# Normalising the finished rows while the last expert still runs, in a decoder layer with mixture of experts

## The chip, the cores and the metric
The kernel runs on one core of a Trainium2 chip. The time is device microseconds (us) of one execution. TensorE (PE) multiplies matrices, with the weight loads listed apart (PEld); VectorE (DVE), ScalarE (ACT) and GpSimd (POOL) do element work; SyncE (SP) issues transfers. POOL also issues the indirect transfers (gather and scatter by a list of row numbers). Engines wait on each other by semaphores only.

## The reference, cut to what matters
64 sequences of 128 tokens, width 256, so 8192 rows. Self attention, residual and layer norm; cross attention, residual and layer norm; then a mixture of experts:

```
probs = softmax(x @ Wr + br); gates, ids = top_k(probs, 2)      # 8 experts, 2 for each token
cap = ceil(1.2 * 8192 / 8) = 1229                                # rows of one expert, by gate, best first
xg = x[disp_tok].reshape(8, cap, 256)
h = silu(xg @ W1 + b1); out = h @ W2 + b2                        # 256 -> 1024 -> 256
y = zeros.at[disp_tok].add(out * gate)
x = layernorm(x + y)                                             # eps 1e-5, no scale or shift
```

A row can be added to by two experts, and by none when both are full. The final norm of a row needs the sum of all its experts.

## The kernel before, in words
The kernel is a row of blocks, and every block ends with all engines meeting. The attention block writes its rows twice to memory: into `rows` (to gather from) and into `total` (to add to). `logits_block` makes the router's logits. `route_block` finds each expert's 1229 rows: a softmax and the two best, a search in 15 steps for each expert's threshold gate (DVE, ACT and PE in turn), running counts, and then in 8 batches one-hot matrices `hit_row` and `hit_lane` whose products give the list `ids`. At its end POOL gathers the first 10 tiles of 128 rows (expert 0, its three chunks) into `xg` (L1292).

`experts_block` takes 8 experts with 3 chunks each (3, 3 and 4 tiles of 128 rows; 384, 384 and 462 rows), 24 chunks in all. Numbers in 32 bits are split into a rounded part and a rest, so each product is three matmuls. TensorE's order for each chunk (L1465 and after) is: transposes of the next chunk (L1448), `up` of this one (48 matmuls), `down` of the chunk before (24 matmuls for each tile of 128 rows). Its last piece is `down` of chunk 23. ACT rounds the transposed rows (L1502), makes silu twice for each of 8 slices (L1531, L1532), and rounds the next expert's weights (L1510). DVE makes the rests (L1559 for rows, L1565 for weights, L1572 for the hidden layer), adds the bias to the result (`take_o`, L1582) and multiplies by the gate (L1587). Two PSUM buffers hold results of `down`, so TensorE's third tile waits until DVE has taken the first. POOL gathers the chunk three ahead (L1623) and adds the finished chunk into `total` by an indirect transfer with addition (`scatter`, L1639). Experts' scatters stay in order, since two may add to the same row.

`norm_block` starts when every scatter has landed. SP loads `total` in 16 groups of 512 rows (L1677), DVE makes the statistics (L1709, L1704), POOL in four small instructions the factor and the shift (L1692 to L1697), ACT normalises 64 tiles (L1718), SP stores 16 groups (L1681).

Of the kernel before, what the change touches and what calls it, by code (L numbers as in the profile page):

```python
# [4 lines left out]
FP32 = mybir.dt.float32  # L5
# [7 lines left out]
P = 128  # L13
# [948 lines left out]
def route_block(nc, tiles, cap, logits, rows_dram, ids, first_weights, first_rows, consts):  # L962
# [7 lines left out]
    PARTS = tiles // BATCH  # L970
    DVE_TAGS = 4
    Q = 2 * tiles
# [3 lines left out]
    with ExitStack() as c:  # L976
# [16 lines left out]
        ident = sb("ident", [P, P])  # L993
# [41 lines left out]
        hit_lane = sb("hit_lane", [P, Q, P], FP16)  # L1035
        hit_row = sb("hit_row", [P, Q, ROWS], FP16)
        tagged = sb("tagged", [P, Q, ROWS], FP16)
# [6 lines left out]
        w1_in, w2_in, w_in = first_weights  # L1044
        xg, x_loaded = first_rows
# [12 lines left out]
        dve_tags = sem("dve_tags")  # L1058
        routed = sem("routed")
# [3 lines left out]
        def _(sp):  # L1063
# [3 lines left out]
            sp.dma_start(w1_in[:], consts["w1"][0:1].rearrange("a (t p) n -> p (a t) n", p=P)).then_inc(w_in, 16)  # L1067
            sp.dma_start(w2_in[:], consts["w2"][0:1].rearrange("a (t p) n -> p (a t) n", p=P)).then_inc(w_in, 16)
# [6 lines left out]
        def _(act):  # L1075
# [3 lines left out]
            nc.scalar.activation(warm[:], dummy[:], ACT.Sign)  # L1079
            act.wait_ge(split, 1)  # L1080
# [7 lines left out]
            for b in range(Q // BATCH):  # L1088
                part, kth = divmod(b, 2)
                if b % DVE_TAGS == DVE_TAGS - 1:  # L1090
                    continue
                act.wait_ge(rows_hit, b + 1)
                for t in range(part * BATCH, (part + 1) * BATCH):
                    q = kth * tiles + t
                    ins = nc.scalar.activation(tagged[:, q, :], hit_row[:, q, :], ACT.Copy, scale=tag[:, t:t + 1])
                ins.then_inc(tags_made, 1)

        @block.tensor
        def _(pe):
# [5 lines left out]
            last.then_inc(pe_done, 1)  # L1105
            for i in range(STEPS):
# [13 lines left out]
            for b in range(Q // BATCH):  # L1120
# [5 lines left out]
                for t in range(part * BATCH, (part + 1) * BATCH):  # L1126
                    q = kth * tiles + t
                    last = nc.tensor.matmul(bi[:, part, :], hit_lane[:, q, :], tagged[:, q, :],
                                            start=(b % 2 == 0 and t == part * BATCH),
                                            stop=(b % 2 == 1 and t == (part + 1) * BATCH - 1))  # L1130
            last.then_inc(pe_done, 1)

        @block.vector
        def _(dve):
# [11 lines left out]
            _, parts, _, _, _ = chunks_of(cap)  # L1146
            v.memset(xg[:, :, parts[-1] - 1, :], 0.0).then_inc(cleared, 1)
            v.memset(ones[:], 1.0)
            v.memset(base[:], 0.0)
            v.memset(ones_h[:], 1.0)  # L1150
            for i in range(STEPS):
                for j in range(3):
                    ins = v.memset(third[:, i, j:j + 1], (j + 1) * step_of(i) - half_unit(i))
            link(ins)
            v.tensor_copy(tries[:], third[:, 0, :])
            link(v.tensor_copy(ahead[:], third[:, 1, :]))

# [30 lines left out]
            dve.wait_ge(pe_done, 1)  # L1188
            v.tensor_copy(gt[:], bt[:]).then_inc(split, 1)
# [69 lines left out]
            for b in range(Q // BATCH):  # L1259
                part, kth = divmod(b, 2)  # L1260
                qs = slice(kth * tiles + part * BATCH, kth * tiles + (part + 1) * BATCH)
                v.tensor_tensor(hit_row[:, qs, :], row_h[:, qs].unsqueeze(2).to_broadcast([P, BATCH, ROWS]),
                                iota_h[:, 0:ROWS].unsqueeze(1).to_broadcast([P, BATCH, ROWS]), ALU.is_equal).then_inc(rows_hit, 1)
                v.tensor_tensor(hit_lane[:, qs, :], lane_h[:, qs].unsqueeze(2).to_broadcast([P, BATCH, P]),
                                iota_h[:].unsqueeze(1).to_broadcast([P, BATCH, P]), ALU.is_equal).then_inc(lanes_hit, 1)
                if b % DVE_TAGS == DVE_TAGS - 1:
                    dve.wait_ge(rows_hit, b + 1)
                    v.tensor_tensor(tagged[:, qs, :], hit_row[:, qs, :],
                                    tag[:, part * BATCH:(part + 1) * BATCH].unsqueeze(2).to_broadcast([P, BATCH, ROWS]),
                                    ALU.mult).then_inc(dve_tags, 1)  # L1270
            dve.wait_ge(pe_done, 4)
# [23 lines left out]


XG = 4
AHEAD = XG - 1


def chunks_of(cap):
# [545 lines left out]
```

## Time and profile before

| | us |
|---|---|
| three runs | 1637.54, 1636.06, 1637.61 (median 1637.54) |
| the profiled execution, its own time | 1637.37 |
| its span, first to last instruction | 1635.6 |
| start of the block of the experts | 1097.6 |
| start of the block of the norm | 1586.4 |

The profile counts its times from the start of the span. An engine's line in a timeline gives the start, the busy time, the engine, the line of the kernel, the operation with what it writes and reads, and how many of them are merged; brackets tell how long the engine had been idle and what ended that. "issue" is a wait for nothing that the profile shows. A line of SPq is a transfer being issued, not its landing.

### The profile page before, as it was taken

Reading aid. Unit: us, or ns where it says so; the run is one execution under the profiler, and the core shown is the slowest. Engines: PE = TensorE matmul, PEld = TensorE weight load, DVE = VectorE, ACT = ScalarE, POOL = GpSimd, SP = SyncE. Lnnn points to the kernel's source line nnn. Section 1 sums busy time; section 2 is a strip of 40 time slices with the busy share of each in tenths; the row PEclk is TensorE's granted clock in tenths of the full one; section 3 lists DMA queues with packets and bytes.
Section 4 is the critical chain, followed back from the end, with each engine's and each line's share of the span. In section 5 each row is a group of like instructions: output and inputs, shape, how many; then the busy total and the mean of one; then the engine's idle time right before and its main releaser. Section 6 shows DMA issues by size and latency. Waiting matters only on the chain. (4 is left out here: it accounts for less than half of the span.)

```text
span 1635.6 us, 43777 instructions
## 1 busy us (share of the span) xinstructions
PE 1412.0 (86%) x17886; PEld 1188.3 (73%) x17886; DVE 1021.5 (62%) x2276; ACT 1015.4 (62%) x1555; POOL 598.8 (37%) x607
## 2 busy tenths in 40 slices
PE   7999999999999999999998560119999999999940
PEld 5777777777777777777776340119999999999940
DVE  5666666666777777777777368955455445445425
ACT  4677777777777777777766352337555456556407
POOL 2645454544433232323230000032455445545236
PEclk9999999999999999999999885559999999999975
DMA  6112122221212222222221451013443444343139
GB/s 189 33 49 62 58 61 60 60 60 60 61 60 73 79 80 78 80 67 82 70 69 45 139 165 15 1 44 82 95 104 47 97 94 95 53 99 48 22 78 355
DMA packets 128006, 129.53 MB, mean 79 GB/s; under 512 B 26496, under 2 KB 114672, under 8 KB 127808
## 3 DMA queue, kind: packets, MB, share of 16 engines
q1 hardware_dynamic: 112704, 106.24, 21.3%
q0 software_dynamic: 15104, 20.48, 7.7%
q8 instruction: 144, 2.36, 0.6%
q14 instruction: 54, 0.44, 0.1%
HBM read 82.53 MB, written 44.16 MB: 77 GB/s over the span
## 5 line engine op out<-in xcount | busy, mean ns | idle before, releaser
L515 ACT ACTIVATE at_pr<-at_A 128x2048 f32<-128x2048 f32 x128 | 240.7, 1880 | 147.2 <-PE at_A L335 147.2
L610 DVE TENSOR_REDUCE at_mx<-at_A 128x12 f32<-128x1536 f32 x128 | 224.6, 1754 | 56.3 <-PE at_A L300 52.7
L35 PE MATMUL ex_D<-ex_w,ex_hT 128*128 128x256 f32 (+1 forms) x1920 | 234.2, 282 | 0.3
L35 PEld LDWEIGHTS ex_D<-ex_w,ex_hT 128*128 128x128 f32 (+1 forms) x1920 | 231.0, 184 | 2.9 <-DVE ex_raw L1582 1.8
L35 PE MATMUL ex_U<-ex_xT,ex_w 128*128 128x384 f32 (+1 forms) x1152 | 224.6, 354 | 3.4 <-DVE ex_xT L1559 3.4
L1639 POOL DMA_INDIRECT total<-ex_o,ids x80 | 131.4, 1642 | 237.1 <-DVE ex_o L1587 220.1
L35 PEld LDWEIGHTS ex_U<-ex_xT,ex_w 128*128 128x128 f32 x1152 | 208.4, 190 | 12.1 <-issue 3.8
L755 POOL TENSOR_SCALAR_AFFINE_SELECT at_pr<-at_pr 128x2048 f32<-128x2048 f32 x64 | 128.5, 2007 | 205.2 <-ACT at_pr L515 205.1
L1572 DVE TENSOR_TENSOR ex_hT<-ex_h,ex_hT 128x384 fp32r<-128x384 f32 (+1 forms) x192 | 112.6, 587 | 100.2 <-ACT ex_hT L1532 90.8
L646 DVE TENSOR_TENSOR at_oT<-at_C,at_oT 128x512 fp32r<-128x512 f32 x64 | 44.2, 691 | 165.3 <-ACT at_oT L528 165.3
L335 PE MATMUL at_A<-at_qp,at_kt 32*128 32x256 f32 x2048 | 139.8, 388 | 0.0
L350 PE MATMUL at_C<-at_pr,at_v 128*32 128x128 f32 x4096 | 138.4, 276 | 1.0 <-ACT at_oq L522 1.0
L350 PEld LDWEIGHTS at_C<-at_pr,at_v 128*32 128x32 f32 x4096 | 104.0, 110 | 43.3 <-issue 42.1
L1531 ACT ACTIVATE ex_h<-ex_U,ex_b 128x384 f32<-128x384 f32 (+1 forms) x192 | 115.9, 604 | 26.7 <-PE ex_U L35 21.4
L1502 ACT CAST ex_xT<-ex_T 128x384 fp32r<-128x384 f32 (+1 forms) x48 | 21.8, 506 | 161.8 <-PE ex_T L1448 161.7
L1532 ACT ACTIVATE ex_hT<-ex_U,ex_b 128x384 fp32r<-128x384 f32 (+1 forms) x192 | 114.3, 595 | 0.0
L762 POOL TENSOR_SCALAR at_shift<-at_mv 128x2 f32<-128x2 f32 x64 | 14.8, 231 | 265.2 <-DVE at_mv L674 262.7
L35 PE MATMUL at_B<-at_wo,at_oT 128*128 128x256 f32 x768 | 108.1, 290 | 1.4 <-DVE at_oT L646 1.4
L1582 DVE TENSOR_TENSOR ex_raw<-ex_D,ex_b 128x256 f32<-128x256 f32 x80 | 33.8, 423 | 118.6 <-PE ex_D L35 118.2
L35 PE MATMUL at_B<-at_wv,at_sT 128*128 128x256 f32 x768 | 106.7, 288 | 0.0
L35 PE MATMUL at_B<-at_sT,at_wk 128*128 128x512 f32 x384 | 105.0, 409 | 0.6 <-ACT at_qp L484 0.6
L1623 POOL DMA_INDIRECT xg<-rows,ids x70 | 92.2, 1318 | 24.1 <-issue 20.1
(219 smaller groups left out, 2690.1 us busy)
## 6 DMA issues: line engine op xcount, KB each, us to landing
w_in<-in_w SPq DMA_DIRECT2D x16, 1024.0 KB
at_turned<-in_x_turned SPq DMA_DIRECT2D x16, 512.0 KB, 4.6
at_x<-in_x SPq DMA_DIRECT2D x16, 512.0 KB, 4.1
x<-at_y SPq DMA_DIRECT2D x32, 256.0 KB, 2.4
at_x<-x SPq DMA_DIRECT2D x16, 512.0 KB, 3.8
at_turned<-in_ctx_turned SPq DMA_DIRECT2D x16, 512.0 KB, 4.8
rows<-at_y SPq DMA_DIRECT2D x32, 256.0 KB, 2.2
total<-at_y SPq DMA_DIRECT2D x32, 256.0 KB, 3.0
```

What stands on the lines that cost most here:

```text
L35: last = nc.tensor.matmul(out, pick_l(left, a), pick_r(right, b), start=(start and n == 0), stop=(stop and n == 2))
L335: last = nc.tensor.matmul(A[:, i, n, :, :], kt[rows, g % 2, half, tok], qp[rows, g % 2, half, :, tok], start=False, stop=(n == 1), skip_gr ...
L350: last = nc.tensor.matmul(b[32 * j:32 * j + VW, (2 * n + quad) * P:(2 * n + quad + 1) * P], v[:, g % 2, 2 * np_ + n, half * HEADS_HALF + 4 ...
L515: nc.scalar.activation(pr[:, k % 2].rearrange("p i n a q -> p (i n a q)"), A[:].rearrange("p i n a q -> p (i n a q)"), ACT.Exp).then_inc(e ...
L610: nc.vector.tensor_reduce(mx[:, k % 2, 0:12], A[:, 0:3].rearrange("p i n a k -> p (i n a) k"), AX, ALU.max).then_inc(max_done, 1)
L646: nc.vector.tensor_tensor(oT[:, u % 2, 1].rearrange("p t n -> p (t n)"), C[1][:, :], oT[:, u % 2, 0].rearrange("p t n -> p (t n)").bitcast ...
L755: nc.gpsimd.affine_select(out=t, in_=t, compare_op=ALU.is_ge, fill=0.0, base=0, pattern=[[0, 16], [1, P]], channel_multiplier=-1).then_inc ...
L1531: nc.scalar.activation(h[:, m % HR, 0:n], U[m % UP][:, 0:n], ACT.Silu, bias=b1[:, j, m:m + 1])
L1532: nc.scalar.activation(hT[:, par(j, ch), 0, m, 0:n], U[m % UP][:, 0:n], ACT.Silu, bias=b1[:, j, m:m + 1]).then_inc(u_done, 1)
L1572: nc.vector.tensor_tensor(hT[:, par(j, ch), 1, m, 0:n], h[:, m % HR, 0:n], hT[:, par(j, ch), 0, m, 0:n].bitcast(FP32), ALU.subtract).then_ ...
L1623: nc.gpsimd.indirect_dma_start(xg[0:n, xg_of(s), b, :], None, rows_dram, bass.IndirectOffsetOnAxis(ap=ids[0:n, e, at:at + 1], axis=0), bou ...
L1639: nc.gpsimd.indirect_dma_start(sum_dram, bass.IndirectOffsetOnAxis(ap=ids[0:n, e, at:at + 1], axis=0), o[0:n, pr, b, :], None, bounds_chec ...
```

## The change
1. The norm's block is gone. Its work stands in the block of the experts. As soon as the scatters of expert 6 have landed (`sum_complete`), SP loads groups 0 to 7 of `total` into eight places (four in the weights' input buffers, two in `o`, two new) and POOL gathers the last expert's own 10 tiles of rows from `total`. The other eight groups are loaded one by one into places whose store has landed. Groups are laid out with four rows side by side in a partition. The groups hold the last expert's rows too, at values that are not final; they are stored and overwritten later.
2. The last expert's results are not scattered into `total`: DVE adds bias, multiplies by the gate and adds to the gathered row (`take_own`), takes statistics of these rows apart, and mixes the statistics of the groups between its pieces.
3. POOL makes the factors, and itself normalises groups 0 to 3; ACT groups 4 to 15 and the own rows. When all 16 stores have landed, POOL scatters the 10 own tiles into `out` (now with 128 spare rows).
4. Expert 0's start stands in `route_block`: weights, biases and the mask are loaded, rounded and split there, and the first chunk is gathered, transposed, rounded and given its gates there. Only two chunks (6 tiles) are gathered in that block; the third follows in the next. Constants are set by POOL and not by DVE at the block's start. The one-hot matrices lie in a ring of 4 batches and no longer all at once; DVE waits before it writes a batch for the products of the batch four before.
5. Weights and the shared buffers are allocated for both blocks. TensorE's `up` and `down` keep their order; the transposes of chunk 0 are what is moved.

```
+            act.wait_ge(sh["w_in"], 32)
+            for src, dst, _ in weights:
+                nc.scalar.copy(dst[:, 0], src[:]).then_inc(sh["w_hi"], 1)
...
+            for k, (src, dst, _) in enumerate(weights):
+                dve.wait_ge(sh["w_hi"], k + 1)
+                v.tensor_tensor(dst[:, 1], src[:], dst[:, 0].bitcast(FP32), ALU.subtract).then_inc(sh["w_lo"], 1)
+            dve.wait_ge(sh["small_in"], 48)
+            dve.wait_ge(x_loaded[0], 16 * parts[0])
...
-            for s in range(AHEAD):
+            for s in range(ROUTED):
...
+            def load_bulk(g):
+                sp.dma_start(space(g), sum_dram[g * G:(g + 1) * G, :].rearrange("(p b) n -> p b n", p=P)).then_inc(bulk_in[g % len(spaces)], 16)
+
+            sum_complete(sp)
+            for g in range(len(spaces)):
+                load_bulk(g)
+            for g in range(groups):
+                if g < POOL_GROUPS:
+                    sp.wait_ge(bulk_made_pool, g + 1)
+                else:
+                    sp.wait_ge(bulk_made_act, g - POOL_GROUPS + 1)
+                sp.dma_start(out_dram[g * G:(g + 1) * G, :].rearrange("(p b) n -> p b n", p=P), space(g)).then_inc(early_stored[g] if g < again else late_stored, 16)
+                if g > 0 and g - 1 < again:
+                    sp.wait_ge(early_stored[g - 1], 16)
+                    load_bulk(g - 1 + len(spaces))
...
+            def take_own(ch, bulk):
+                e, j = E - 1, (E - 1) % 2
+                dve.wait_ge(own_in[ch], 16 * parts[ch])
+                dve.wait_ge(gate_ready, e * NC + ch + 1)
+                for b, (_, n) in enumerate(tiles_of[ch]):
+                    at = tiles_before(e, ch) + b
+                    dve.wait_ge(d_full, at + 1)
+                    if b == 0:
+                        wait(dve, own_sum, starts[ch])
+                    nc.vector.tensor_tensor(raw[0:n, b, :], Dn[(starts[ch] + b) % 2][0:n, :], b2[0:n, j, :], ALU.add).then_inc(d_done, 1)
+                    dve.wait_ge(d_done, at + 1)
+                    nc.vector.scalar_tensor_tensor(total_rows(ch, b, n), raw[0:n, b, :], gate[0:n, ch, b:b + 1], total_rows(ch, b, n),
+                                                   ALU.mult, ALU.add).then_inc(own_sum, 1)
+                    bulk_statistics(*bulk[b])
...
+                    elif ch == 1:
+                        rest_h(e, j, ch)
+                        take_own(0, ((0, 4), (4, 8), (8, 12)))
+                        own_statistics(0)
+                    else:
+                        for m in range(HT):
+                            rest_h(e, j, ch, m, m + 1)
+                            bulk_statistics(12 + m, 13 + m)
+                        take_own(1, ((20, 24), (24, 28), (28, 32)))
+                        own_statistics(1)
+                        take_own(2, ((32, 36), (36, 40), (40, 44), (44, tiles)))
+                        own_statistics(2)
...
+            sum_complete(pool)
+            for ch in range(NC):
+                free = (E - 1) * NC + ch
+                pool.wait_ge(t_full, free * 2)
+                pool.wait_ge(gate_ready, free)
+                for b, (_, n) in enumerate(tiles_of[ch]):
+                    at = starts[ch] + b
+                    nc.gpsimd.indirect_dma_start(total_rows(ch, b, n), None, sum_dram,
...
             for g in range(groups):
...
+                pool.wait_ge(bulk_stats, g + 1)
+                rates(g * NB, NB, bulk_rates)
+                if g < POOL_GROUPS:
+                    pool.wait_ge(bulk_rates, g + 1)
+                    for b in range(NB):
+                        t = g * NB + b
+                        ins = nc.gpsimd.tensor_scalar(space(g)[:, b, :], space(g)[:, b, :], rstd[:, t:t + 1], shift[:, t:t + 1],
+                                                      ALU.mult, ALU.add)
+                    ins.then_inc(bulk_made_pool, 1)
+                for ch in range(NC - 1):
+                    if g == OWN_AFTER[ch]:
+                        own_rows(ch)
+            own_rows(NC - 1)
+            for g in range(again):
+                pool.wait_ge(early_stored[g], 16)
+            pool.wait_ge(late_stored, 16 * (groups - again))
+            for ch in range(NC):
+                pool.wait_ge(own_made, ch + 1)
...
+                    nc.gpsimd.indirect_dma_start(out_dram, bass.IndirectOffsetOnAxis(ap=ids[0:n, E - 1, at:at + 1], axis=0),
+                                                 total_rows(ch, b, n), None, bounds_check=out_dram.shape[0] - 1).then_inc(own_stored, 16)
+            pool.wait_ge(own_stored, 16 * LT)
```

Here POOL_GROUPS is 4, OWN_AFTER is (4, 7), ROUTED is 2, `again` is 8 (16 groups, 8 places).

## Rows read from the trace of the kernel before

**Rows 1.** Busy time by stage: start:end, length, busy of each engine, granted clock, DMA share, GB/s

```profile
1105.40:1571.60 466.20, 465.85 (x3226) 454.64 (x3226) 227.09 (x453) 256.87 (x445) 211.32 (x143) 0.99 0.37 74
1571.60:1586.40 14.80, 0.00 (x0) 0.00 (x0) 1.47 (x5) 0.00 (x0) 6.16 (x4) 0.59 0.28 33
1586.40:1635.60 49.20, 0.00 (x0) 0.00 (x0) 26.81 (x128) 32.10 (x64) 27.22 (x65) 0.50 1.02 342
```

**Rows 2.** Timeline at the start of the routing block

```profile
976.34 0.63 ACT L1078 ACTIVATE rt_probs<-rt_probs 128x512 f32<-128x512 f32 x1 [7.08 <-DMA rt_limits<-in_limits]
992.28 0.63 ACT L1081 ACTIVATE rt_low<-rt_gt 128x512 f32<-128x512 uint16 x1 [15.22 <-DVE rt_gt L1189]
```

**Rows 3.** Timeline from the end of routing to the first product of expert 0

```profile
1080.81 0.24 DVE L1280 TENSOR_TENSOR ids<-rt_id_sum,rt_empty 128x80 int32<-128x80 f32 x1
1082.09 1.32 POOL L1292 DMA_INDIRECT xg<-rows,ids  x1 [162.52 <-SPq L976]
1094.26 1.03 POOL L1292 DMA_INDIRECT xg<-rows,ids  x1 [0.30 <-issue]
1097.63 3.70 ACT L1510 CAST ex_w<-w_in 128x2048 fp32r<-128x2048 f32 x2 [23.85 <-PEq L976]
1099.56 4.49 DVE L1565 TENSOR_TENSOR ex_w<-w_in,ex_w 128x2048 fp32r<-128x2048 f32 x2 [18.50 <-ACT ex_w L1510]
1099.70 3.04 POOL L1623 DMA_INDIRECT xg<-rows,ids  x1 [0.30 <-issue]
1100.50 1.54 PE L1448 MATMUL ex_T<-ex_ident,xg 128*128 128x128 f32 x6 [23.15 <-DMA ex_ident<-in_ident]
1103.04 1.90 POOL L1623 DMA_INDIRECT xg<-rows,ids  x1 [0.30 <-issue]
1104.28 1.01 DVE L1559 TENSOR_TENSOR ex_xT<-ex_T,ex_xT 128x384 fp32r<-128x384 f32 x2
1105.43 6.56 PE L35 MATMUL ex_U<-ex_xT,ex_w 128*128 128x384 f32 x24 [3.39 <-DVE ex_xT L1559]
```

**Rows 4.** Timeline of the last expert: scatters and one instruction of each kind

```profile
1531.18 1.73 POOL L1639 DMA_INDIRECT total<-ex_o,ids  x1 [0.30 <-issue]
1532.87 8.69 PE L35 MATMUL ex_D<-ex_w,ex_hT 128*128 128x256 f32 x72
1552.94 0.64 DVE L1572 TENSOR_TENSOR ex_hT<-ex_h,ex_hT 128x462 fp32r<-128x462 f32 x1 [0.62 <-ACT ex_hT L1532]
1568.81 0.42 DVE L1582 TENSOR_TENSOR ex_raw<-ex_D,ex_b 128x256 f32<-128x256 f32 x1 [2.42 <-PE ex_D L35]
1573.08 1.56 POOL L1639 DMA_INDIRECT total<-ex_o,ids  x1 [6.08 <-DVE ex_o L1587]
1578.67 1.48 POOL L1639 DMA_INDIRECT total<-ex_o,ids  x1 [0.31 <-issue]
1586.46 19.35 SPq L1677 DMA_DIRECT2D nm_x<-total  x16
```

**Rows 5.** Timeline of the norm: one group on DVE, POOL and ACT, and the stores

```profile
1592.17 1.37 DVE L1709 BATCH_NORM_STATS2 nm_stats<-nm_x 128x6 f32<-128x256 f32 x4
1592.44 0.24 POOL L1692 TENSOR_SCALAR nm_shift<-nm_mv 128x4 f32<-128x4 f32 x1 [5.86 <-DVE nm_mv L1704]
1593.58 0.38 DVE L1704 BATCH_NORM_AGGREGATE nm_mv<-nm_stats 128x2 f32<-128x6 f32 x4
1594.42 32.10 ACT L1718 ACTIVATE nm_x<-nm_x,nm_shift,nm_rstd 128x256 f32<-128x256 f32 x64 [41.51 <-POOL nm_shift L1697]
1594.47 0.24 POOL L1692 TENSOR_SCALAR nm_shift<-nm_mv 128x4 f32<-128x4 f32 x1
```

**Rows 6.** POOL's costliest groups in the span: count, then busy us and mean ns

```profile
L755 POOL TENSOR_SCALAR_AFFINE_SELECT at_pr<-at_pr 128x2048 f32<-128x2048 f32 x64 | 128.5, 2007 | 205.2 <-ACT at_pr L515 205.1
L746 POOL TENSOR_TENSOR at_sT<-at_turned,at_sT 128x1024 fp32r<-128x1024 f32 x32 | 76.4, 2387 | 53.3 <-DVE at_m L620 35.4 <-ACT at_sT L471 17.9
```

**Rows 7.** Chain that ended last: start, length, what

```profile
1586.46 3.95 DMA nm_x<-total
```

More of the change, by code:

```diff
@@ L959, in _, with route_block @@
             take(groups - 1)
-def route_block(nc, tiles, cap, logits, rows_dram, ids, first_weights, first_rows, consts):
+def route_block(nc, tiles, cap, logits, rows_dram, ids, sh, consts):
     LT = -(-cap // P)
@@ L970, in route_block @@
     PARTS = tiles // BATCH
+    _, parts, starts, widths, tiles_of = chunks_of(cap)
     DVE_TAGS = 4
+    RING = 4
     Q = 2 * tiles
@@ L1092, in _ @@
                 act.wait_ge(rows_hit, b + 1)
-                for t in range(part * BATCH, (part + 1) * BATCH):
-                    q = kth * tiles + t
-                    ins = nc.scalar.activation(tagged[:, q, :], hit_row[:, q, :], ACT.Copy, scale=tag[:, t:t + 1])
+                for k in range(BATCH):
+                    t = part * BATCH + k
+                    ins = nc.scalar.activation(tagged[:, b % RING, k, :], hit_row[:, b % RING, k, :], ACT.Copy, scale=tag[:, t:t + 1])
                 ins.then_inc(tags_made, 1)
+            for half in range(HALVES):
+                act.wait_ge(sh["t_full"], half + 1)
+                nc.scalar.copy(xT[:, 0, 0, half, :widths[0]], T[half][:, 0:widths[0]]).then_inc(sh["x_hi"], 1)
         @block.tensor
@@ L1125, in _ @@
                     pe.wait_ge(dve_tags, (b + 1) // DVE_TAGS)
[L1126 to L1131, printed above, removed]
+                for k in range(BATCH):
+                    last = nc.tensor.matmul(bi[:, part, :], hit_lane[:, b % RING, k, :], tagged[:, b % RING, k, :],
+                                            start=(b % 2 == 0 and k == 0), stop=(b % 2 == 1 and k == BATCH - 1))
+                last.then_inc(batch_done, 1)
+            pe.wait_ge(x_loaded[0], 16 * parts[0])
+            for half in range(HALVES):
+                for k, (off, n) in enumerate(tiles_of[0]):
+                    last = nc.tensor.matmul(T[half][:, off:off + n], xg[0:n, 0, k, half * P:(half + 1) * P], ident[0:n, 0:n],
+                                            start=True, stop=True, is_transpose=True)
+                last.then_inc(sh["t_full"], 1)
         @block.vector
@@ L1145, in _ @@
             v = nc.vector
[L1146 to L1156, printed above, removed]
             link(v.tensor_reduce(col[:], logits[:], AX, ALU.max))
@@ L1297 @@
 XG = 4
+NC_CHUNKS = 3
 AHEAD = XG - 1
+ROUTED = 2
+POOL_GROUPS = 4
+OWN_AFTER = (4, 7)
+SPARE = 2
 def chunks_of(cap):
     LT = -(-cap // P)
-    NC = 3
+    NC = NC_CHUNKS
     used = cap + cap % 2
@@ L1341, in experts_block @@
-        gate = sb("gate", [P, NC, NB])
         raw = sb("raw", [P, NB, D])
         o = sb("o", [P, 2, NB, D])
-        ident = sb("ident", [P, P])
-        T = [c.enter_context(nc.psum_tensor(f"ex_T{i}", [P, G], FP32)) for i in range(2)]
+        groups = tiles // NB
+        stats = sb("stats", [P, tiles + LT, 6])
+        mv = sb("mv", [P, tiles + LT, 2])
+        rstd = sb("rstd", [P, tiles + LT])
+        shift = sb("shift", [P, tiles + LT])
+        minus_half = sb("minus_half", [P, NB])
@@ L1394, in landed, with space, total_rows, own_at @@
             return 16 * sum(parts[t % NC] for t in range(s % 2, s + 1, 2))
+        def space(g):
+            return spaces[g % len(spaces)]
+        def total_rows(ch, b, n):
+            return xg[0:n, xg_of((E - 1) * NC + ch - 1), b, 0:D]
+        def own_at(ch):
+            return tiles + starts[ch]
+        def sum_complete(eng):
+            last = (E - 1) * NC - 1
+            for s in (last - 1, last):
+                eng.wait_ge(added[s % 2], landed(s))
         def gathered(s):
@@ L1641, in scatter @@
                                                  compute_op=ALU.add).then_inc(added[pr], 16)
-            for s in range(E * NC):
+            for s in range(ROUTED, AHEAD):
+                gather(s)
+            nc.gpsimd.memset(minus_half[:], -0.5).then_inc(half_made, 1)
+            for s in range((E - 1) * NC + 1):
                 if s + AHEAD < E * NC:
```

281 lines of the change are left out of this document (159 added, 122 removed).

## The prediction

> **What bounds the kernel now.** I read the busy time by stage first. From 1105.4 to 1571.6 us PE is busy 465.85 of 466.20 us; nothing in the experts can be gained except work of PE itself, and the change removes none. Behind it come two stages without PE: 14.8 us to the norm (only 6.16 us of POOL in them) and 49.2 us of norm with the DMA engines full (share 1.02, 342 GB/s) [rows 1]. That is 64.0 us after PE's end, for 16.8 MB of loads and stores and one scatter. In the experts' stage the DMA share is 0.37, DVE is busy 49%, ACT 55% and POOL 45%: there is room for the norm beside PE, if the sums are complete early enough. The timeline before the experts comes next: `ids` are done at 1081.05, PE's first product starts at 1105.43, 24.4 us later. In them POOL issues ten gathers, all engines meet, and ACT, DVE and PE prepare expert 0 in turn [rows 3].
>
> **Part A, the start of expert 0.** At the front of routing nothing is gained: ACT's exponential waits for the tenth constant's landing at 976.34, whatever DVE clears before [rows 2]. POOL's constants stand beside that. The two rounding copies (3.70 us [rows 3]) move to ACT between 976.97 and 992.28, when it was idle for 15.2 us [rows 2]; if the weights came over 11 us late there, the search would start late. The ring's wait costs nothing as long as PE stays less than three batches behind DVE, which the busy PE of those products cannot miss: I count 0, bounds 0 and +1.
> After `ids`: before, ten gathers from 1082.09 to 1095.29, then the meeting, 2.34 us until ACT starts at 1097.63 [rows 3]. After the change six gathers. The steps of their pitch are (1094.26 - 1082.09)/9 = 1.35 us, but DVE now splits the weights (4.49 us) at 1081.1 to 1085.6, and beside just this work two gathers took 3.04 and 1.90 us and not 1.0 [rows 3]. So: two gathers until about 1086.6, four more to 1092.0. The third ends at 1088, its rows are there some 2 us later, six transposes (1.54), the last rounding (0.5) and the rests (1.01) [rows 3] end at 1092.8. The meeting, 2.3 us: PE's first product at 1095.1 instead of 1105.4. I take **-10.5 us** (1094.9). Bounds: gathers not held by DVE and the meeting at 1090.3 give -12.3; all six held for 0.3 us more each, -8.5. The four gathers of the third chunk now stand at the front of the next block, to 1100.3. PE has the first chunk's 48 products before it asks for them (24 of them took 6.56 us [rows 3]), so they are in time by some microseconds. The second expert's weights wait for them too, with most of an expert's length in hand.
> The Trainium skill, SBUF — State Buffer, section Who interferes with whom, says that a VectorE instruction with two SBUF inputs holds off a GpSimd instruction that reads SBUF until it ends. The 3.04 us agree with it. By it POOL's four normalised groups and DVE's rests (both inputs in SBUF) would hold each other off too, by at most 8 x 0.6 = 5 us in the stage below; the sum goes without.
>
> **Part B, the tail.** Times here are those of the profile before; part A shifts them all.
> 1. The sums are complete when expert 6's last scatter has landed. Its issue ends at 1531.18 + 1.73 = 1532.9. The last scatter of all ended at 1580.15 and the next block began at 1586.46 [rows 4]; less the 2.3 us of a meeting [rows 3] it landed 4.0 us after. So 1536.9.
> 2. POOL gathers ten own tiles: 10 x 1.35 + 0.8 for waits = 14.3 us, to 1551.2. The first three land at about 1544.2 (issue 4.3, landing 3, an estimate between the 2 us above and the 4.0).
> 3. PE stalls. DVE takes `down` of chunk 21 only with the own rows there; PE's 72 products start at 1532.87, at 2.9 us for a tile [rows 4], and the third tile waits from 1538.6 to 1544.6. That is 6 us, and the granted clock was down to 0.59 on average in the stage after PE's end [rows 1], so some 2 us more after it. It is later held by DVE again and ends near 1579.7, 8 us late. It does not set the end, by the next steps.
> 4. DVE from 1544.2: 26.8 us for 16 groups of statistics [rows 1], own statistics 10 x 0.44 = 4.4 [rows 5], bias and multiply-add 10 x 0.84 = 8.4 and eight rests 8 x 0.64 = 5.1 [rows 4]: 44.7 us, to 1589 without gaps, 1591.7 with those where a tile of PE is late. Group 15 is done before its own last four tiles, at 1589.8.
> 5. POOL from 1551.2, once group 0's statistics are there at 1546.7. One set of four small instructions has a pitch of 1594.47 - 1592.44 = 2.03 us [rows 5]; 19 sets are 38.4. Normalising on POOL is not in the trace. Bounds: 0.25 us a tile (2007 ns / 8) and 0.60 (2387 / 4) [rows 6], I take 0.35, nearer the first, which also has one tile as input: 16 x 0.35 + 0.3 = 5.9. POOL ends its last set at 1595.4, two us behind group 15's at 1593.4.
> 6. ACT: a tile is 32.10 / 64 = 0.50 us [rows 5]; group 15 at 1595.4, its store issued and landed 4.4 us later (3.95 for the first load [rows 7]): 1599.8. The own last tiles are ready at 1597.4. The loads of groups 8 to 15 hang on stores 0 to 7; they are issued by 1586 and do not bind. The 16.8 MB need 49 us at 342 GB/s [rows 1] and have 63.
> 7. POOL's ten scatters wait for all stores. With addition the pitch is (1578.67 - 1573.08)/3 = 1.86 us [rows 4]; the gather without it has 1.35. A plain scatter is in no row: bounds 1.31 and 1.86, I take 1.40, as only the addition divides them: 14.0, to 1613.8. Landing 3.9 as in step 1: **1617.7**.
> So the tail ends 1635.6 - 1617.7 = 17.9 us earlier. Both parts: 1635.6 - 17.9 - 10.5 = 1607.2 of span; the profiled execution is 1.8 us over its span, **1609.0 us**. It stands 0.2 us under the median of the three runs, so that is a gain of 28.5 us on the median, 1.7%.
>
> **Rivals.**
> (a) The own rows come late. The gathers share the DMA engines with eight loads of 512 KB, which fill them for 12 us at 342 GB/s. If they land behind these (own rows at 1553, not 1544), DVE becomes the bound: its 44.7 us from there give 1598 for group 15, 5.3 + 4.4 us on to the stores, scatters from 1607.7: **1617**. Half way, 1614. For it: the gathers of 3.04 us [rows 3] show that POOL's transfers can be held. Against: the stores of the same queue come only later. The Trainium skill, DMA: Bandwidth & Descriptors, section Queues, rings and completion order, says that an engine serves its queues in turn, by packets; that speaks for the shorter landing, and no row here shows the two side by side.
> (b) The plain scatter costs as much as the adding one: + 10 x 0.46 = 4.6 us, **1613.6**. With POOL's tiles at 0.60 another 4, 1617.6.
> (c) The changed start gives nothing, as the meeting waits for something else (the third gather's rows, or code): **1619.5**.
> (d) Slower: POOL is the serial engine of the new tail, and all 16 tiles that it normalises stand before every other step of it. Each us more for a tile costs 16 us at the end. At 2.2 us a tile (a small instruction, POOL held off by DVE) the sum is 1609 + 16 x 1.85 = **1638.6**; it decides from 2.15. Against: 2048 elements took 2.0 us while DVE ran beside [rows 6], and this is 256.
> (e) That the change does not do what it says: TensorE's order is said to be changed, and in the code it stays. Nothing is priced for it; it is no case of its own.
>
> **How the numbers follow.** The forecast 55%, (a) 18%, (b) 15%, (c) 6%, (d) 3%, 3% for something faster: POOL's tiles at 0.25, gathers not held, a landing of 2 us give 1609 - 1.6 - 1.8 - 1.9 = 1603.7. The bounds of the unknown costs together reach from there to 1609 + 4 + 4.6 + 5 + 2 = 1624.6. The range is 1602 to 1624. About 0.2%, 3.3 us, is what a measurement of this kernel can tell from no change: faster 0.95, the same 0.01, slower 0.04.
>
> **What would show it.** In the profile after: PE's first product 10 us earlier, with six gathers before it, the first two long; a hole in PE of some 6 us in the last expert, with a lower granted clock behind it, and PE's end 8 us later in its stage; POOL busy without a gap from there to its last set, then a wait for the stores of 4 to 5 us, then ten scatters at 1.3 to 1.9 us, which end the chain. Step 4 is wrong if the chain runs through DVE's statistics, step 6 if through ACT or the stores' loads. The whole is wrong if POOL's tiles take over 1 us.

## The result, and the profile after

| | before | after |
|---|---|---|
| median | 1636.8 us (4 runs, 1636.03 to 1637.61) | 1614.8 us (4 runs, 1612.23 to 1615.79) |
| ratio | | 0.9863, 95% interval 0.9846 to 0.988 |
| the profiled execution, its own time | 1637.37 | 1615.76 |
| its span | 1635.6 | 1614.0 |

The gain is 22.0 us (28.5 were forecast); the forecast was 1609.0 us with a range of 1602 to 1624. A repeat in a later measurement gave 1614.03 us beside 1637.91.

The attention stage takes a few us more or less from one execution to the next: the first load of the routing block starts at 970.27 us in the profile before, at 972.33 in the one after and at 968.42 in the repeat. So times of different executions are compared from that load and written with a plus: +123.8 is 123.8 us after it. By this clock before ends at +665.3, after and its repeat at +641.7 both.

The busy time by stage of the kernel after, columns as in [rows 1]: the experts to PE's end, then to the first scatter into `out`, then to the end.

```profile
1096.10:1571.70 475.60, 466.97 (x3226) 454.99 (x3226) 250.34 (x553) 264.28 (x462) 246.54 (x210) 0.99 0.41 96
1571.70:1594.80 23.10, 0.00 (x0) 0.00 (x0) 11.39 (x54) 20.92 (x42) 16.38 (x38) 0.56 0.85 313
1594.80:1614.00 19.20, 0.00 (x0) 0.00 (x0) 0.00 (x0) 0.00 (x0) 9.92 (x10) 0.50 0.19 66
```

PE has the same work (466.97 us against 465.85) and 8.6 us of holes. Behind its end stand 42.3 us and not 64.0 [rows 1]; in the first 23.1 of them ACT is the busy engine (20.92 us), in the last 19.2 only POOL issues.

The timeline of the kernel after from `ids` to the first product of expert 0 answers to [rows 3].

```profile
1082.79 0.24 DVE L1289 TENSOR_TENSOR ids<-rt_id_sum,rt_empty 128x80 int32<-128x80 f32 x1
1082.94 4.49 DVE L1292 TENSOR_TENSOR ex_w_even<-ex_w_in,ex_w_even 128x2048 fp32r<-128x2048 f32 x2
1084.06 2.35 POOL L1321 DMA_INDIRECT ex_xg<-rows,ids  x1 [108.56 <-issue]
1086.71 1.62 POOL L1321 DMA_INDIRECT ex_xg<-rows,ids  x1 [0.30 <-issue]
1088.63 1.01 POOL L1321 DMA_INDIRECT ex_xg<-rows,ids  x1 [0.30 <-issue]
...
1091.44 1.54 PE L1146 MATMUL ex_T<-ex_ident,ex_xg 128*128 128x128 f32 x6 [12.13 <-DMA ex_xg<-rows,ids]
1092.57 1.01 POOL L1321 DMA_INDIRECT ex_xg<-rows,ids  x1 [0.30 <-issue]
1092.89 1.20 DVE L1301 TENSOR_TENSOR ex_xT<-ex_T,ex_xT 128x384 fp32r<-128x384 f32 x2 [1.00 <-ACT ex_xT L1108]
1096.11 1.30 PE L35 MATMUL ex_U<-ex_xT,ex_w_even 128*128 128x384 f32 x3 [3.13 <-PEq L978]
```

`ids` to PE's first product: 13.1 us, before 24.4. Two gathers run beside DVE's split of the weights and take 2.35 and 1.62 us, the others 1.01; the sixth ends at 1093.58, and the meeting is over 2.5 us later. The transposes and rests lie beside the last gathers.

The tail of the kernel after, from its timelines, in order of start; this answers to [rows 4, 5].

```profile
1522.99 1.73 POOL L1803 DMA_INDIRECT total<-ex_o,ids  x1 [0.30 <-issue]
1526.76 1.75 SPq L1523 DMA_DIRECT2D ex_w_in<-total  x4
1527.56 1.12 POOL L1822 DMA_INDIRECT ex_xg<-total,ids  x1 [2.85 <-issue]
1530.33 1.01 POOL L1822 DMA_INDIRECT ex_xg<-total,ids  x1 [0.30 <-issue]
1536.68 0.42 DVE L1718 TENSOR_TENSOR ex_raw<-ex_D,ex_b 128x256 f32<-128x256 f32 x1 [10.16 <-DMA ex_xg<-total,ids]
1537.16 4.54 PE L35 MATMUL ex_D<-ex_w_odd,ex_hT 128*128 128x256 f32 x24 [6.62 <-issue]
1539.54 1.02 POOL L1822 DMA_INDIRECT ex_xg<-total,ids  x1 [0.30 <-DVE ex_mv L1697]
1542.97 2.18 POOL L1849 TENSOR_SCALAR ex_w_in<-ex_w_in,ex_rstd,ex_shift 128x256 f32<-128x256 f32 x4
1547.52 3.26 POOL L1849 TENSOR_SCALAR ex_w_in<-ex_w_in,ex_rstd,ex_shift 128x256 f32<-128x256 f32 x4
1551.68 20.00 PE L35 MATMUL ex_D<-ex_w_odd,ex_hT 128*128 128x256 f32 x168
1562.53 2.08 ACT L1642 ACTIVATE ex_o<-ex_o,ex_shift,ex_rstd 128x256 f32<-128x256 f32 x4 [9.48 <-POOL ex_shift L1836]
1584.33 1.41 DVE L1692 BATCH_NORM_STATS2 ex_stats<-ex_spare 128x6 f32<-128x256 f32 x4 [2.25 <-DMA ex_spare<-total]
1590.97 2.07 ACT L1634 ACTIVATE ex_xg<-ex_xg,ex_shift,ex_rstd 128x256 f32<-128x256 f32 x4
1594.81 1.15 POOL L1863 DMA_INDIRECT out<-ex_xg,ids  x1 [3.87 <-issue]
1606.50 0.97 POOL L1863 DMA_INDIRECT out<-ex_xg,ids  x1 [0.30 <-issue]
```

To be seen: the last scatter of expert 6 ends at 1524.72, and SP is released at 1526.76. The third own gather ends at 1531.34, its rows are there at 1536.66. PE stands for 6.62 us, and the 24 matmuls behind the hole take 4.54 us where 2.9 is usual [rows 4]. ACT gets its first group at 1562.53. The first scatter stands at 1594.81, ten take 12.66 us, and the span ends 6.5 us behind the last one.

What PE does in and behind that hole, from the busy time by stretch (start:end, length, PE busy, granted clock, DMA share, GB/s):

```profile
1530.54:1537.16 6.62, 0.00 (x0) 0.73 1.02 394
1537.16:1541.54 4.38, 4.38 (x24) 0.63 1.02 399
```

The granted clock was 1.00 in the stretch before the hole, 0.63 on average in the 4.38 us behind it, and 1.00 again from 1541.54 on. So the slow 24 matmuls go with a lower clock, as forecast.

The end of the chain of waits of the kernel after (start, us, what):

```profile
1574.71 0.21 POOL ex_shift L1836
1574.92 0.03 issue
1574.94 8.09 ACT ex_w_in L1642 x16
1583.03 4.01 ACT ex_o L1642 x8
1587.04 4.01 ACT ex_spare L1642 x8
1591.05 0.02 issue
1591.07 2.67 DMA out<-ex_spare
```

Up to 1574.9 the chain runs through POOL, from there through ACT without a gap. The prediction had named this, the chain through ACT, as the sign that its step 6 is wrong. POOL's groups in the span of the kernel after (busy us, mean ns, idle before) answer to the bounds of [rows 6]:

```profile
L1849 POOL TENSOR_SCALAR ex_w_in<-ex_w_in,ex_rstd,ex_shift 128x256 f32<-128x256 f32 x16 | 10.4, 660 | 0.4
L1822 POOL DMA_INDIRECT ex_xg<-total,ids x10 | 10.3, 1025 | 5.6 <-issue 5.3 <-DVE ex_mv L1697 0.3
L1863 POOL DMA_INDIRECT out<-ex_xg,ids x10 | 9.9, 992 | 6.6 <-issue 6.6
```

### The profile page after: what moved, and what is told of

Same layout as the page of the kernel before. It is cut to its first block and busy times, and to the rows that moved or that the text cites. A ratio compares the mean times of both kernels' runs of the same rounds, so it can differ in the third digit from the quotient of the medians.

```text
span 1614.0 us, 43834 instructions
## 1 busy us (share of the span) xinstructions
PE 1415.6 (88%) x17886; PEld 1190.3 (74%) x17886; DVE 1026.1 (64%) x2246; ACT 1011.6 (63%) x1549; POOL 621.5 (39%) x696
## 5 line engine op out<-in xcount | busy, mean ns | idle before, releaser
L755 POOL TENSOR_SCALAR_AFFINE_SELECT at_pr<-at_pr 128x2048 f32<-128x2048 f32 x64 | 128.4, 2007 | 205.2 <-ACT at_pr L515 205.2
L1803 POOL DMA_INDIRECT total<-ex_o,ids x70 | 115.8, 1655 | 197.3 <-DVE ex_o L1736 182.4
L35 PE MATMUL ex_D<-ex_w_odd,ex_hT 128*128 128x256 f32 (+1 forms) x960 | 118.3, 284 | 6.9 <-issue 6.6
L35 PEld LDWEIGHTS ex_D<-ex_w_odd,ex_hT 128*128 128x128 f32 (+1 forms) x960 | 116.6, 186 | 8.2 <-issue 6.8
L35 PE MATMUL ex_D<-ex_w_even,ex_hT 128*128 128x256 f32 (+1 forms) x960 | 117.2, 281 | 1.0 <-DVE ex_raw L1731 0.9
L35 PEld LDWEIGHTS ex_D<-ex_w_even,ex_hT 128*128 128x128 f32 (+1 forms) x960 | 115.2, 184 | 2.7 <-DVE ex_raw L1731 2.2
L35 PE MATMUL ex_U<-ex_xT,ex_w_even 128*128 128x384 f32 (+1 forms) x576 | 113.5, 356 | 3.8 <-PEq L978 3.1
L35 PEld LDWEIGHTS ex_U<-ex_xT,ex_w_even 128*128 128x128 f32 x576 | 104.9, 191 | 8.6 <-issue 3.5
L35 PE MATMUL ex_U<-ex_xT,ex_w_odd 128*128 128x384 f32 (+1 forms) x576 | 111.0, 351 | 0.0
```

The source lines that it names most:

```text
L35: last = nc.tensor.matmul(out, pick_l(left, a), pick_r(right, b), start=(start and n == 0), stop=(stop and n == 2))
L755: nc.gpsimd.affine_select(out=t, in_=t, compare_op=ALU.is_ge, fill=0.0, base=0, pattern=[[0, 16], [1, P]], channel_multiplier=-1).then_inc ...
L1803: nc.gpsimd.indirect_dma_start(sum_dram, bass.IndirectOffsetOnAxis(ap=ids[0:n, e, at:at + 1], axis=0), o[0:n, pr, b, :], None, bounds_chec ...
```

## The experiments

Three measurements of four kernels each, every one with runs of the kernel before beside them, to which the ratios refer; the kernel after stood at 0.9863 and in the first of these measurements at 0.9856 (0.9841 to 0.9871; called the repeat below). Experiments 1 to 3 were measured beside the repeat, 4 to 7 and 8 to 11 later; their medians are set against its 1614.03 us too, and the kernel before had 1637.91, 1637.13 and 1636.35 us in the three.

The traces have a width of their own. In kernels that are the same up to there, the issue of expert 6's last scatter ends at +552.2 to +552.5 in four traces (after, repeat, experiments 8 and 9) and at +553.5 to +553.7 in five (2, 3, 4, 5 and 7). Of a later end in these five, about 1.2 us stood there before the tail began.

**1. The start alone.** Part A as in the change, with the norm's block and the last expert's end as before.

```
-            sum_complete(sp)
-            for g in range(len(spaces)):
-                load_bulk(g)
...
-            sum_complete(pool)
...
+            scatter(E * NC - 1)
...
+    norm_block(nc, tiles, total, out)
```

> Only the changed start of expert 0 (point 4 of the change); the norm is its own block again after the last scatter, as in the kernel before. Theory: the start is worth 11.4 us from the routing block's first instruction to the first product of expert 0 (123.8 us in the profile after, 135.2 before), of which 1.1 are lost again in the first expert, so 1636.8 - 10.3 = 1626.5 us, and the distance from the last product to the end is 64 us as before. Rival (c), the start gives nothing: 1637. A third reading, that the start is worth less and the tail more than the forecast said: between, 1630.

Measured: 1628.19 us, ratio 0.9944 (0.9929 to 0.9959). Part A is worth 9.7 us (10.5 forecast), and the tail 14.2 more (to the repeat's 1614.03), where 17.9 were forecast. The expectation of 1626.5 was 1.7 us too low. In the traces the way from the routing block's first load to the first product is 123.7 us here, 123.8 in the change and 135.2 before: 11.4 us. Some of it is lost again in the first expert, where PE waits for ACT's `ex_hT` and DVE's `ex_raw`: PE has holes of 1.20, 0.52 and 0.90 us here, 0.63 and 0.89 in the profile after, 0.60 in the repeat, none before.

**2. Twice as many groups on POOL.**

```
-POOL_GROUPS = 4
-OWN_AFTER = (4, 7)
+POOL_GROUPS = 8
+OWN_AFTER = (8, 10)
```

> POOL normalises 8 groups instead of 4 (and ACT 8 instead of 12); own rows' factors come after groups 8 and 10. Theory that POOL's serial chain sets the tail: 16 more tiles of 0.55 to 0.8 us, so the end comes 9 to 13 us later, about 1625 us. Rival, DVE's statistics and the loads they wait for set the tail: those have 3 us in hand, so up to 1618. Rival, ACT sets it: ACT has 16 tiles less, so the same or 2 us faster, 1613.

Measured: 1623.77 us, 0.9914 (0.9899 to 0.9929): 9.7 us dearer than the repeat of the change for 16 tiles more, 0.61 us a tile. Two lines of its timeline, POOL's last tiles and ACT's first:

```profile
1575.32 2.16 POOL L1849 TENSOR_SCALAR ex_spare<-ex_spare,ex_rstd,ex_shift 128x256 f32<-128x256 f32 x4
1579.52 2.07 ACT L1642 ACTIVATE ex_w_in<-ex_w_in,ex_shift,ex_rstd 128x256 f32<-128x256 f32 x4 [26.60 <-POOL ex_shift L1836]
```

ACT, which needs 0.50 us a tile and has time, waits 26.6 us for the factors that stand behind POOL's tiles. In these 16 tiles more, what POOL normalises stays on the path with its full price.

**3. The last wait on SP.** SP and not POOL waits for the ten scatters into `out`.

```
-            pool.wait_ge(own_stored, 16 * LT)
+            sp.wait_ge(own_stored, 16 * LT)
```

> The final wait for the ten scattered tiles stands on SP and not on POOL. In the profile after, the last scatter is issued at 1607.5, the DMA engines are idle from 1609, the span ends at 1614.0. Theory 1, that what follows a wait of POOL for its transfers costs some 4.3 us until all engines have met: POOL comes to the end while the rows land, so 2 us faster than the changed kernel, 1612.8. Theory 2, that the 5 us are the landing itself (receipts of writes): no change, 1614.8.

Measured: 1613.33 us, 0.985 (0.9836 to 0.9863), 0.7 us under the repeat, which the times alone can't tell from nothing. The traces can: from the end of the last issue to the end of the span it is 4.95 us here, 4.9 and 5.0 in the two later kernels with this edit, and 6.5 to 6.6 in all eight traces that have the scatters and not this edit (after, its repeat, experiments 2, 4, 5, 6, 8 and 9). So 1.6 us of the 6.5 hang on the wait's standing on POOL. The last line of POOL in this trace:

```profile
1608.17 0.98 POOL L1864 DMA_INDIRECT out<-ex_xg,ids  x1 [0.30 <-issue]
```

The span of this execution ends at 1614.1, and by the common clock at +641.7 like the change: POOL's last set is done 1.6 us later here (+620.3), which hides the gain. What the 1.6 us consist of is not shown. In the kernel after SP and POOL both wait for the landing of expert 6's scatters, and POOL's first gather starts 0.80 us behind SP's first load (1527.56 and 1526.76), so POOL's later release is at most half of it; what POOL still has to do behind the wait before the engines meet may be the rest.

**4. Factors for two groups at once.** POOL's set of four small instructions takes 8 columns for the groups 4 to 13: five sets fewer.

```
+                if POOL_GROUPS <= g < groups - 2:
+                    if g % 2 == 0:
+                        pool.wait_ge(bulk_stats, g + 2)
+                        rates(g * NB, 2 * NB, bulk_rates)
...
```

> POOL makes the factors for two groups in one set of four instructions (groups 4 to 13; 14 and 15 stay single), so 5 sets fewer. If POOL's chain without a gap sets the end (in the changed kernel's trace it is busy from 1540.63 to 1590.94, 2.0 us a set), each pair saves about 1.3 us, 6.5 us in all, until DVE's statistics of group 15 (1586.15) bind: the scatters start 3 to 4 us earlier, about 1610.5 us, ratio to the kernel before 0.983 and to the changed one 0.9975. If DVE or the loads set the end, 0 to -1 us: 1613 to 1615, and the pair's wait for the later group may cost 1 us.

Measured: 1613.86 us, 0.9856 (0.984 to 0.9872). Nothing; its trace ends at +644.0, of the 2.3 us more some 1.2 stood before the tail. The timeline of this kernel shows POOL waiting where it had not waited:

```profile
1572.86 0.24 POOL L1831 TENSOR_SCALAR ex_shift<-ex_mv 128x8 f32<-128x8 f32 x1 [2.23 <-DVE ex_mv L1698]
1578.18 0.24 POOL L1831 TENSOR_SCALAR ex_shift<-ex_mv 128x8 f32<-128x8 f32 x1 [2.74 <-DVE ex_mv L1698]
1583.60 1.41 DVE L1693 BATCH_NORM_STATS2 ex_stats<-ex_spare 128x6 f32<-128x256 f32 x4 [2.43 <-DMA ex_spare<-total]
```

POOL waits for DVE and DVE for the loads. POOL's gapless chain was not what alone set the end.

**5. Own rows before the loads.**

```
             sum_complete(sp)
+            sp.wait_ge(own_in[0], 16 * parts[0])
             for g in range(len(spaces)):
```

> SP begins the eight loads of the sums only when the last expert's first three own tiles have landed. If the loads held up the own rows (they landed 5.3 us after the third gather's issue), these land about 2 to 3 us sooner and the hole in TensorE (6.62 us) is 2 to 3 us shorter; the loads come 7 us later. If POOL's chain sets the end, the time stays within 1 us of 1614. If the late own rows set the end (rival a of the forecast), 2 us or more faster, 1612 or less. If the loads bind, 2 to 5 us slower. If the landing is slow for a reason of its own, the hole stays at 6 us or more.

Measured: 1613.88 us, 0.9861 (0.9845 to 0.9877): the same as the change. The timeline of it:

```profile
1527.74 1.01 POOL L1823 DMA_INDIRECT ex_xg<-total,ids  x1 [0.31 <-issue]
1530.55 0.42 DVE L1719 TENSOR_TENSOR ex_raw<-ex_D,ex_b 128x256 f32<-128x256 f32 x1 [6.60 <-DMA ex_xg<-total,ids]
1531.03 4.63 PE L35 MATMUL ex_D<-ex_w_odd,ex_hT 128*128 128x256 f32 x24 [3.06 <-DVE ex_raw L1719]
```

The first 4.27 us of these 24 matmuls, as a stretch:

```profile
1531.03:1535.30 4.27, 4.27 (x23) 0.60 0.87 294
```

Without the loads beside them the rows are there 1.8 us after the third issue and not 5.3; PE's hole is 3.06 us and not 6.62. Rival (a) had its mechanism, at 3.5 us, and had nothing to say on the end. The edit moves two things at once, since the loads now start at +562.1 and not at +554.4. But POOL's first tile starts 18.0 us behind the last scatter here and 18.2 us in the kernel after: POOL's own ten gathers stand before it, not the own rows' landing or PE's hole.

**6. The exponential first.** In the routing block ACT takes its exponential ahead of its wait for the ten constants.

```
-            act.wait_ge(const_in, 160)
             act.wait_ge(routed, 1)
             nc.scalar.activation(pr[:, :, :], pr[:, :, :], ACT.Exp).then_inc(act_done, 1)
+            act.wait_ge(const_in, 160)
```

> In the routing block ACT takes its first exponential ahead of its wait for the ten constants. In the changed kernel's trace DVE stands idle for 5.17 us ahead of it. If that wait is all, the stretch from the routing block's first load to the first product of expert 0 falls from 123.8 to about 121.2 us and the time by 2.6 us, to 1611.5. If the next step needs a constant as late anyway, nothing: 1614.

Measured: 1611.48 us, 0.9842 (0.9828 to 0.9855), 2.5 us under the repeat (2.3 by the ratios, whose intervals still overlap a little); first load to first product 121.3 us instead of 123.8. Its timeline:

```profile
970.80 0.63 ACT L1083 ACTIVATE rt_probs<-rt_probs 128x512 f32<-128x512 f32 x1 [2.50 <-DVE rt_probs L1164]
975.38 0.17 DVE L1170 CAST rt_limits_h<-rt_limits 128x3 f16<-128x3 f32 x1 [1.92 <-DMA rt_limits<-in_limits]
```

Of DVE's 5.17 us of waiting 0.69 remain, the exponential itself, and 1.92 come back a few instructions later, where the constants are needed. The 2.5 us are sure at the first product only: this execution ends at +641.1, 0.6 us before the change. Its last scatter of expert 6 is issued by +551.0, 1.4 us before that of the change and 2.5 us before those of the later five traces, so how much of the gain reaches the end lies within the width of the traces.

**7. No scatter into `out`.** The ten scatters and their wait are left out, so the last expert's rows keep values that are not final.

```
...
-                    nc.gpsimd.indirect_dma_start(out_dram, bass.IndirectOffsetOnAxis(ap=ids[0:n, E - 1, at:at + 1], axis=0),
-                                                 total_rows(ch, b, n), None, bounds_check=out_dram.shape[0] - 1).then_inc(own_stored, 16)
-            pool.wait_ge(own_stored, 16 * LT)
+            pool.wait_ge(own_made, NC)
```

> The ten scatters of the last expert's rows into the output and the wait for them are left out; POOL waits for all stores and for the own rows and ends. In the changed kernel ten issues take 12.8 us from 1594.81 and the span ends 6.5 us after the last. If the end belongs to the wait for POOL's own transfers, the span from the routing block's first load is 641.7 - 12.8 - 6.5 + 2.3 (a meeting) to the point where the stores are done, about 624.5 us, and the time 1597. If the 6.5 us come at any end of the program, 641.7 - 12.8 = 628.9 and 1601.

Measured: 1598.47 us (2 runs), 0.9762 (0.9744 to 0.978), 15.6 us under the repeat, between the two theories. The trace says the same: the span ends 3.4 us after the point where the first scatter would stand (1590.72, POOL's end, + 3.87). So, as an estimate from this one trace, of the 6.5 us in the kernel after some 3.4 come without any scatter too, and 3.1 belong to the scatters' landing and POOL's wait for it.

**8. A ninth place for the groups.** The buffer of chunk 23's gathered rows is free by then; it becomes a place, and a load waits for the store nine groups earlier.

```
-        spaces += [o[:, k] for k in range(2)] + [spare[:, k] for k in range(SPARE)]
+        spaces += [o[:, k] for k in range(2)] + [spare[:, k] for k in range(SPARE)] + [xg[:, (E * NC - 1) % XG, :, 0:D]]
...
+                if g == len(spaces) - 1:
+                    sp.wait_ge(t_full, 2 * E * NC)
+                    sp.wait_ge(gate_ready, E * NC)
```

> A ninth place for a group of the sums (the buffer of the gathered rows of chunk 23, free once they are transposed), so that a load waits for the store nine groups before and not eight. DVE's waits for loads at groups 13 to 15 (1.47, 0.70 and 2.25 us in the changed kernel's trace) should be gone or below 1 us. If POOL's gapless chain alone sets the end, nothing comes of it: 1613 to 1615. If the loads set it, 3 us or more: 1611.

Measured: 1612.35 us beside 1636.35, 0.9854 (0.9839 to 0.9869): nothing, since the repeat has 0.9856. DVE's waits for loads are gone and its last group is done at +609.8 instead of +613.8, but the first scatter stands at +622.3 as against +622.5:

```profile
1590.24 1.15 POOL L1866 DMA_INDIRECT out<-ex_xg,ids  x1 [3.84 <-issue]
```

The loads alone don't set the end either.

**9. Nine places and pairs.** Both edits above.

> The ninth place and the factors for two groups at once, together. Theory: POOL's chain and the chain of store, load and statistics end within 3 us of each other, so neither change alone brings much (the pairs alone: 1613.9) and both together 4 to 5 us: POOL's last set ends about 5 us sooner after the routing block's first load than in the changed kernel, 1609.5. Rival: something third (ACT, the stores) stands at the same place: within 1 us of 1613.9.

Measured: 1612.21 us, 0.985 (0.9835 to 0.9865). My theory of 4 to 5 us fell: with both chains shortened POOL's last set is done 4.0 us sooner (+614.6), and the first scatter only 0.8 (+621.7). The timelines of this kernel show the third one:

```profile
1560.87 2.09 ACT L1646 ACTIVATE ex_o<-ex_o,ex_shift,ex_rstd 128x256 f32<-128x256 f32 x4 [10.11 <-POOL ex_shift L1840]
1584.18 0.20 POOL L1840 TENSOR_TENSOR ex_shift<-ex_shift,ex_rstd 128x4 f32<-128x4 f32 x1
1587.67 2.08 ACT L1637 ACTIVATE ex_xg<-ex_xg,ex_shift,ex_rstd 128x256 f32<-128x256 f32 x4
1591.50 1.16 POOL L1872 DMA_INDIRECT out<-ex_xg,ids  x1 [7.12 <-issue]
```

POOL is done at 1584.4 and waits 7.12 us. ACT works without a gap from 1560.87 to 1589.75: 28.9 us for 48 tiles of groups and 10 of its own. It starts at +591.1, as in the kernel after (+590.2), since the factors of group 4, ACT's first, stand behind the tiles that POOL normalises itself. From there ACT's own work is as long as POOL's.

**10 and 11. Everything together, with four and with two groups on POOL.** Nine places, pairs, the exponential first, the last wait on SP, the own rows before the third load; in the second kernel also `POOL_GROUPS = 2`, the last two lines of the diff.

```
+                if g == 2:
+                    sp.wait_ge(own_in[0], 16 * parts[0])
...
-POOL_GROUPS = 4
+POOL_GROUPS = 2
```

> The ninth place, the pairs, ACT's exponential before its wait for the constants (-2.6 measured alone), the last wait on SP instead of POOL (-0.7), and the own rows before the third load of the sums (alone 0; DVE begins 2 us sooner with it). If they add: 1609.5 - 2.6 - 0.7 and up to -2 for the last: 1604 to 1606.5. If the last only moves the wait to the loads: 1606.5.

> As e11_all, but POOL itself normalises groups 0 and 1 only, ACT 2 to 15. POOL's chain is 5.3 us shorter, ACT's 4.1 us longer. If POOL's tiles (0.55 to 1.0 us each, forecast 0.35) still lie on the path, 1 to 3 us faster than e11; if DVE's 45 us from the own rows' landing set the end by now, the same; if ACT becomes the bound, 1 to 4 us slower.

Measured: 1607.87 us, 0.9824 (0.9811 to 0.9838), and 1605.69 us, 0.9808 (0.9794 to 0.9821). The first is over the 1604 to 1606.5 that were expected: in its trace the first scatter comes 3.7 us sooner than in the change (2.5 of them stand at the first product already), and the end behind the last issue is 1.6 us shorter. The second is the fastest kernel of this study, 30.7 us under the kernel before. Its timelines:

```profile
1550.23 4.08 ACT L1649 ACTIVATE ex_w_in<-ex_w_in,ex_shift,ex_rstd 128x256 f32<-128x256 f32 x8 [3.12 <-POOL ex_shift L1843]
1583.74 2.07 ACT L1640 ACTIVATE ex_xg<-ex_xg,ex_shift,ex_rstd 128x256 f32<-128x256 f32 x4
1587.55 1.16 POOL L1875 DMA_INDIRECT out<-ex_xg,ids  x1 [6.27 <-issue]
```

ACT begins at +579.1 and not at +588.2 as with four groups; it has 4 us more to do and 2.4 us of waits for POOL's factors, and the first scatter comes at +616.4 instead of +618.8. So eight tiles fewer on POOL, 5.3 us by the expectation, gave back about 2.2 us and not their full price. The 2.2 us between the two medians are about the measurement's own width; the traces agree with them. Not tried: four groups on POOL, but with the factors of group 4 made ahead of them.

## Why the prediction was right, and where it was off

The time fell inside the range, 5.8 us over the forecast, and the main steps are in the trace: TensorE's hole, its late end that is off the path, POOL's chain without a gap, the ten scatters last. The number alone speaks as well for two rivals, (b) with 1613.6 us and half of (a) with 1614, and neither was the cause: a plain scatter has a pitch of 1.28 us, and the own rows' landing is off the path (experiment 5). By the common clock, forecast and measured:

| point | forecast | measured |
|---|---|---|
| first product | +124.6 | +123.8 |
| sums complete (step 1) | +556.1 | +554.4 |
| own gathers issued (2) | +570.4 | +568.2 |
| first own rows there (2) | +563.4 | +564.3 |
| PE's end (3) | +598.9 | +599.4 |
| group 15's statistics (4) | +609.0 | +613.8 |
| POOL's last set (5) | +614.6 | +618.6 |
| first scatter (6) | +619.0 | +622.5 |
| last scatter issued (7) | +633.0 | +635.1 |
| end | +636.9 | +641.7 |

The remaining 2 us between forecast and profile are the attention stage's own.

**Part A** gave 11.4 us against 10.5, with the two slow gathers as read from [rows 3]; 9.7 in the time, as PE has holes of 0.6 to 2.6 us in the first expert in the traces with this start. The forecast had no such hole; that ACT and DVE start that expert with less in hand is my reading, and no run tests it. Rival (c) is out, by experiment 1.

**Step 1.** The landing is 2.04 us, not 4.0. I had worked it out from the norm's start in [rows 4] less a meeting of 2.3; but there POOL stood at the wait for its own scatters (1580.15 to 1586.46). By experiment 3 an end with such a wait on POOL is 1.6 us dearer than one with it on SP. The inference most likely took this for landing; it gave 2 us too many here, and at the end 3.9 us where 6.5 were needed.

**Step 2.** The own rows took 5.3 us to land beside the loads, 1.8 alone (experiment 5), against my 3. The Trainium skill, DMA: Bandwidth & Descriptors, section Queues, rings and completion order, has each engine take turns between its queues by packets. I read that as a short landing; the runs show that with loads of 512 KB queued beside them 384 rows land 3.5 us later. That this comes from such turns is not shown. This costs the end nothing.

**Steps 3 and 4.** PE's hole was 6.62 us (6 forecast), its end at +599.4. DVE's work was as counted, but it waited 4.4 us for the last loads; step 6 had said they do not bind. They don't bind the end (experiment 8), but they bound DVE, and with it POOL in experiment 4.

**Step 5 is where most of the error lies.** 16 tiles of normalising took 10.4 us, mean 0.66, where I had taken 0.35 from 2048 elements in 2.0 us [rows 6]. Dividing a long instruction by its length leaves out what each short one costs; the bound of 0.60 was nearer, and still low. The Trainium skill, GPSIMD Engine Reference, section Performance versus the Vector engine, gives at best 1.8 cycles an element at 1.2 GHz: 0.38 us for 256 elements is an estimate of the floor from it, without the dispatch of the instruction; my 0.35 stood under it. But this case's trace does not agree with that figure as a floor: the instruction of 2048 elements in [rows 6] took 2007 ns, where 1.8 cycles an element would be 3.07 us, an estimate from the same section. So it is no floor for every instruction here. The shortest tile here is 0.55 us. Beside DVE's rests a group takes 3.26 us instead of 2.18; the Trainium skill, SBUF — State Buffer, section Who interferes with whom, names that hold, and the trace agrees: against 2.18 us it was worth 1.1 us in that group and 0.4 in the next, where I had set it at up to 5 in all and left it out. The 19 sets took 39.9 us with the gaps instead of 38.4.

POOL started 2.2 us sooner than forecast, took 6.2 more, the stores 0.5 less, ten scatters 1.3 less and the end 2.6 more: 4.8 us. Errors of 8.8 us one way and 4.0 the other stand behind the small sum; that they partly cancel is luck.

**Step 6** had ACT's last tiles two us behind POOL's last set, and there they were (1593.04 and 1590.94). But I read ACT as a follower, and by the prediction's own sign the step is wrong: the chain of waits ends in ACT's groups from 1574.9 on. Experiments 4, 8 and 9 show three chains of the same length: sets on POOL at 2.0 us a group, groups on ACT at 2.0 us, and the circle of store, load and statistics. What precedes all three, and what the path holds at full price, is POOL's first four groups, by the times of ACT's first group; experiment 2 pays 0.61 us for each tile more, and experiment 11 gets about 2.2 us back for eight tiles fewer. That is rival (d)'s lever at a size of 0.66 us and not of 2.15.

**Step 7.** The plain scatter takes 0.97 us and has a pitch of 1.28, so that rival (b) (1.86) is out; the adding one takes 1.66 on average. The end behind it is 6.5 us: some 3.4 that come without scatters too (experiment 7), and 3.1 for the landing with POOL's wait.

**(e)** TensorE's order is the same in both traces: `up`, `down` of the chunk before, and 168 matmuls of `down` at the end.

## What to carry to other kernels

When one engine makes what another needs, its own share of the bulk work has to stand behind the other's first input, not ahead of it: what precedes the first release can lie on the path, however idle the waiting engine looks (here 0.61 us for each tile added, and 2.2 us back for eight taken away). When a chain without a gap is shortened and nothing comes of it, look for the engine that ran at the same pitch behind it; only shortening both, or starting both sooner, moves the end. Take the price of a short instruction from a short one: a long one divided by its length was a lower bound here (0.25 us against 0.55 at the shortest).

## What of the hardware was not expected

- An indirect transfer of 128 rows of 1 KB costs POOL 1.01 us as a gather, 0.97 as a plain scatter and 1.66 as an adding one (`total`, mean of 70), with 0.30 us between two.
- With the last wait for POOL's own transfers on POOL the program ends 1.6 us later than with it on SP (6.5 to 6.6 us against 4.9 to 5.0 from last issue to end, eight traces against three). For one landing that both engines wait for, POOL starts its next transfer 0.80 us after SP.
- POOL's power of 128x8 takes 1.67 us and of 128x4 1.04: small as they are, 0.63 of the 1.04 us goes by the number of columns.
- 24 matmuls behind a hole of 6.62 us took 4.54 us, behind one of 3.06 us 4.63, at granted clocks of 0.63 and 0.60: the shorter stop cost as much afterwards.
